# A residual pair of normalised 3x3 convolutions: another layout of the image, halos by GpSimd, another order on ScalarE, sixteen transfers per image

## The reference

```
g  = groupnorm(x), 8 groups of 2 channels, over a whole image, no affine part
k  = einsum('lj,lk,li->ijkl', u, w, v)        # 3 x 3 x 16 x 16 from three factors
x  = x + relu(conv3x3(g, k, padding SAME) + b)
```

## Time and profile before

| | before |
|---|---|
| median of 3 runs | 6190.59 us |
| the profiled execution | 6208.09 us |
| its span, first to last instruction | 6206.2 us |
| mean granted TensorE clock | 0.917 |
| HBM read, written | 268.72 MB, 268.44 MB |

### The profile page before, as it was taken

One profiled execution on the slowest core, in us unless ns is written; L12 is line 12 of the kernel. 1 busy time (PEld: TensorE's weight loads), 2 busy tenths in 40 slices (PEclk: granted clock), 3 DMA queues, 4 the chain that ended last, 5 costly groups with the idle time before them and its releaser, 6 DMA issues.

```text
span 6206.2 us, 285409 instructions
## 1 busy us (share of the span) xinstructions
PE 5071.9 (82%) x137088; PEld 2751.6 (44%) x137088; DVE 2693.6 (43%) x3084; ACT 2328.8 (38%) x3202; POOL 972.6 (16%) x453
## 2 busy tenths in 40 slices
PE   5888888888888888888888888888888878888887
PEld 3444444444444444444444444444444444444444
DVE  3444444444444444444444444444444444444443
ACT  3343343433333334334334343343433434334342
POOL 2111110111111111111111011110111101111110
PEclk9999998999999998999999899999999999999998
DMA  4454445444444445445444454454444544445424
GB/s 93 97 109 95 89 100 110 91 92 93 105 102 89 92 100 108 92 90 111 99 89 95 97 108 92 89 107 98 95 92 90 110 96 93 92 93 111 96 62 87
DMA packets 186931, 597.41 MB, mean 96 GB/s; under 512 B 13360, under 2 KB 54704, under 8 KB 185776
## 3 DMA queue, kind: packets, MB, share of 16 engines
q1 hardware_dynamic: 116144, 310.70, 23.2%
q10 hardware_dynamic: 69632, 268.45, 20.8%
HBM read 268.72 MB, written 268.44 MB: 87 GB/s over the span
## 4 chain that ended last, share of the span: by engine, by line
PE 68%; issue 19%; ACT 6%; DVE 3%; ACTq 2%; DMA 1%; POOL 0%; SPq 0%; DVEq 0%; POOLq 0%
PE ps_y L300 30%; PE ps_y L253 21%; PE ps_x L326 10%; ACT junk L356 5%; PE ps_x L281 5%; DVE odds L491 2%; ACTq L404 2%; PE ps_y L258 1%; PE ps_x L223 1%; ACT relu L374 1%; PE ps_y L261 0%; ACT relu L377 0%; PE ps_x L233 0%; DMA raw<-in_x 0%; DMA out<-pixels 0%
## 5 line engine op out<-in xcount | busy, mean ns | idle before, releaser
L300 PE MATMUL ps_y<-odds,scaled 32*32 32x512 f32 x49152 | 2021.2, 655 | 269.9 <-issue 230.3
L253 PE MATMUL ps_y<-evens,scaled 32*32 32x512 f32 x48384 | 1936.1, 638 | 350.8 <-issue 331.9
L300 PEld LDWEIGHTS ps_y<-odds,scaled 32*32 32x32 f32 x49152 | 892.4, 107 | 1163.0 <-issue 755.4
L491 DVE TENSOR_TENSOR odds<-ps_x,relu 128x2048 f32<-128x2048 f32 x256 | 586.9, 2293 | 1886.2 <-PE ps_x L281 1100.7
L253 PEld LDWEIGHTS ps_y<-evens,scaled 32*32 32x32 f32 x48384 | 927.0, 106 | 1054.4 <-issue 654.4
L491 DVE TENSOR_TENSOR result<-ps_x,relu 128x2048 f32<-128x2048 f32 x256 | 586.6, 2292 | 1314.1 <-PE ps_x L326 477.9
L211 POOL TENSOR_TENSOR fold<-fold,evens 128x1024 f32<-128x1024 f32 x384 | 843.8, 2197 | 837.4 <-DVE evens L481 800.4
L281 PE MATMUL ps_x<-evens,constants 32*32 32x512 f32 x16384 | 877.3, 652 | 117.0 <-issue 117.0
L326 PE MATMUL ps_x<-odds,constants 32*32 32x512 f32 x16384 | 838.3, 638 | 102.4 <-issue 102.2
L377 ACT ACTIVATE relu<-ps_y,bias 128x2048 f32<-128x2048 f32 x256 | 503.6, 1967 | 1070.1 <-PE ps_y L300 1070.1
L356 ACT ACTIVATE junk<-odds 128x1024 f32<-128x1024 f32 x512 | 544.4, 1063 | 928.2 <-DVE odds L491 639.4
(11 more groups left out here) (42 smaller groups left out, 1146.3 us busy)
## 6 DMA issues: line engine op xcount, KB each, us to landing
raw<-in_x SPq DMA_DIRECT2D x256, 1024.0 KB, 15.0
out<-pixels ACTq DMA_DIRECT2D x256, 1024.0 KB, 14.2
odds<-odds SPq DMA_DIRECT2D x64, 384.0 KB, 17.7
evens<-evens SPq DMA_DIRECT2D x64, 96.0 KB, 2.1
odds<-odds SPq DMA_DIRECT2D x64, 96.0 KB, 18.1
evens<-evens SPq DMA_DIRECT2D x64, 32.0 KB, 2.1
odds<-odds SPq DMA_DIRECT2D x64, 32.0 KB, 16.3
parameters<-in_params SPq DMA_DIRECT2D x2, 96.5 KB, 2.0
```

The source lines that it names most:

```text
L253: done = nc.tensor.matmul(ps_y[part, r, :], w0[rows, t * Q:(t + 1) * Q], N0[rows, k:k + EACH, i:i + H], start=(t == 0), stop=(t == NTAP - 1))
L300: done = nc.tensor.matmul(ps_y[Q * r:Q * (r + 1), q, :], w1[p % 2][Q * q:Q * (q + 1), t * Q:(t + 1) * Q], t1[Q * q:Q * (q + 1), r, k:k + E ...
L491: nc.vector.tensor_tensor(to, ps_x[:].rearrange("p q (k h) -> p q k h", h=H), R[n % R_SLOTS][:], ALU.add).then_inc(added, 1)
```

## The change

A quadrant now holds a quarter of the height: 64 rows of all 128 pairs, so `raw` has one pair of rows per partition (32 KB, contiguous in memory), `evens` is 129 slots by 66 rows and `odds` 33 slots by 258 rows. A round covers 8 slots of 64 rows in place of 2 of 256; four rounds stay. `turn_in` and `turn_out` make two transposes per round, one for each row of the pair, and write or read every second element; a ninth transpose per image brings the wrap-around slot. The halos of the evens are then rows above and below (six copies by GpSimd), those of the odds the last slot (four copies); no DMA is left in them. Padding of the evens is two instructions on 32 partitions. In the first round of conv0 four of 16 places have a slot split off. Squares are four instructions of some 2048 elements per image and kind in place of eight of 1024; on ScalarE each relu now stands ahead of the squares of its round, `pad_evens` and the roots behind a relu. There is one relu buffer, and relu waits for the add before. On VectorE `scale_weights` stands behind the add and `turn_out` of its round. Loads and stores are both issued by SP: sixteen transfers per image and direction, each over every sixteenth partition (8 partitions of 32 KB), in pieces of at most 256 elements (`max_dma_last_dim=RUN`).

```diff
+PAIRS = W // 2
+SLOTS = PAIRS // QUADS
+EACH = 8
+ROUNDS = SLOTS // EACH
+HQ = H // QUADS
+HALVES = 2
 HP = H + 2
-EACH = 2
-ROUNDS = SLOTS // EACH
-HB = H // Q
-RUN = W // QUADS * C
+HQP = HQ + 2
+WIDE = EACH * HQ
+ROW = W * C
+RUN = 256
 BANK = 512
-R_SLOTS = 2
 COUNT = H * W * 2
 NTAP = SIDES * TAPS
-FOLDS = SLOTS - 1
+FOLDS = 2 * ROUNDS - 1
+FOLD = EACH // 2
 
 PRM = Q * (1 + SIDES + TAPS) + 1
 CST = Q * (SIDES + SIDES + 1) + 2
 
-IN_DMAS, OUT_DMAS, HALO0_DMAS, HALO1_DMAS = QUADS, QUADS, 2, 3
+STRIDE = 16
+IN_DMAS, OUT_DMAS = STRIDE, STRIDE
+TURNS = HALVES * ROUNDS + 1
+HALO0, HALO1 = 2 * (QUADS - 1), QUADS
 ODDS_SUM, ODDS_PAD = 1, 2
-EVENS_SUM = 2
-EVENS_IN_A = {2: (1,), 3: (2, 3)}
-EVENS_IN_B = {0: (4,), 1: (5, 6, 7), 2: (8,)}
+EVENS_SUM, EVENS_PAD = 2, 3
 HOOK_AFTER = 2
 
 
...
 
-        raw = sb("raw", [P, HB, RUN])
-        N0 = sb("evens", [P, QUADS * SLOTS + 1, HP])
-        T1 = [sb(f"odds{i}", [P, QUADS, SLOTS + 1, HP]) for i in range(2)]
-        T2 = sb("result", [P, QUADS, EACH, H])
-        pixels = sb("pixels", [P, HB, RUN])
...
+        T1 = [sb(f"odds{i}", [P, SLOTS + 1, HP]) for i in range(2)]
+        T2 = sb("result", [P, QUADS, EACH, HQ])
+        pixels = sb("pixels", [P, HALVES, ROW])
+        R = sb("relu", [P, QUADS, WIDE])
+        fold = sb("fold", [P, QUADS, FOLD * HQ])
+        junk = sb("junk", [P, QUADS, WIDE + HQ])
         par = [sb(f"parameters{y}", [P, PRM]) for y in range(2)]
         cst = sb("constants", [P, CST])
         w_plain = [sb("weights0", [P, (2 * NTAP + 2) * Q]), sb("weights1", [P, (NTAP + 1) * Q])]
         w0 = sb("scaled0", [P, (2 * NTAP + 2) * Q])
         w1 = [sb(f"scaled1{i}", [P, (NTAP + 1) * Q]) for i in range(2)]
         mixed = sb("mixed", [P, SIDES, Q])
-        zeros = sb("zeros", [P, 2 * QUADS * (SLOTS + 1)])
-        acc = [sb(f"partial{y}", [P, SLOTS]) for y in range(2)]
+        zeros = sb("zeros", [P, PAIRS + 1])
+        acc = [sb(f"partial{y}", [P, ROUNDS]) for y in range(2)]
...
+                    pool.wait_ge(halo0, HALO0 * p + 2 * r + 1)
+                    nc.gpsimd.tensor_copy(N0[below, :, 0], N0[above, :, HQ]).then_inc(halo0, 1)
 
             def halo_of_odds(p):
-                sp.wait_ge(added, round_of(0, p, 0) + 1)
+                pool.wait_ge(added, round_of(0, p, 0) + 1)
+                pool.wait_ge(halo0, HALO0 * (p + 1))
                 t = T1[p % 2]
-                inner = slice(1, 1 + H)
-                sp.dma_start(t[0:P - Q, :, SLOTS, inner], t[Q:P, :, 0, inner]).then_inc(halo1, 16)
-                sp.dma_start(t[P - Q:P, 0:QUADS - 1, SLOTS, inner], t[0:Q, 1:QUADS, 0, inner]).then_inc(halo1, 16)
-                sp.dma_start(t[P - Q:P, QUADS - 1, SLOTS, inner], t[0:Q, 0, 0, inner]).then_inc(halo1, 16)
-
-            load(0)
+                for q in range(QUADS):
+                    of = (q + 1) % QUADS
+                    if q:
+                        pool.wait_ge(halo1, HALO1 * p + q)
+                    nc.gpsimd.tensor_copy(t[Q * q:Q * (q + 1), SLOTS, 1:1 + H],
...
+            folds(0)
             halo_of_evens(0)
-            load(1)
             for p in range(IMAGES):
                 halo_of_odds(p)
                 if p + 1 < IMAGES:
+                    folds(p + 1)
                     halo_of_evens(p + 1)
-                if p + 2 < IMAGES:
-                    load(p + 2)
-
-        @block.gpsimd
-        def _(pool):
-            nc.gpsimd.memset(zeros[:], 0.0).then_inc(zeros_set, 1)
-
-            def chunk(d):
-                return N0[:, d::SLOTS, 1:1 + H]
-
-            for p in range(IMAGES):
-                for d in range(2, SLOTS + 1):
-                    pool.wait_ge(turned_in, SLOTS * p + d)
-                    if d == 2:
-                        if p:
-                            pool.wait_ge(reduced0, p)
-                    else:
-                        pool.wait_ge(folded, FOLDS * p + d - 2)
-                    nc.gpsimd.tensor_tensor(fold[:], chunk(1) if d == 2 else fold[:], chunk(d),
-                                            ALU.add).then_inc(folded, 1)
 
         @block.tensor
...
+                            if f or q:
                                 done = nc.tensor.matmul(ps_y[part, r, :], w0[rows, t * Q:(t + 1) * Q],
-                                                        N0[rows, k:k + EACH, i:i + H],
+                                                        N0[rows, k:k + EACH, i:i + HQ],
                                                         start=(t == 0), stop=(t == NTAP - 1))
                             else:
                                 at = NTAP + 2 + t
-                                nc.tensor.matmul(ps_y[part, r, 0:H], w0[rows, at * Q:(at + 1) * Q],
-                                                 N0[rows, k, i:i + H],
+                                nc.tensor.matmul(ps_y[part, r, 0:HQ], w0[rows, at * Q:(at + 1) * Q],
+                                                 N0[rows, k, i:i + HQ],
                                                  start=(t == 0), stop=False, skip_group_check=True)
-                                nc.tensor.matmul(ps_y[part, r, H:EACH * H], w0[rows, t * Q:(t + 1) * Q],
-                                                 N0[rows, k + 1, i:i + H],
+                                nc.tensor.matmul(ps_y[part, r, HQ:WIDE], w0[rows, t * Q:(t + 1) * Q],
+                                                 N0[rows, k + 1:k + EACH, i:i + HQ],
                                                  start=False, stop=False, skip_group_check=True)
                                 if t == 0:
-                                    nc.tensor.matmul(ps_y[part, r, 0:H], w0[rows, (NTAP + 1) * Q:(NTAP + 2) * Q],
-                                                     center[0][rows, :].to_broadcast([Q, H]),
+                                    nc.tensor.matmul(ps_y[part, r, 0:HQ], w0[rows, (NTAP + 1) * Q:(NTAP + 2) * Q],
...
                             k = EACH * f + side
                             done = nc.tensor.matmul(ps_y[Q * r:Q * (r + 1), q, :],
                                                     w1[p % 2][Q * q:Q * (q + 1), t * Q:(t + 1) * Q],
-                                                    t1[Q * q:Q * (q + 1), r, k:k + EACH, i:i + H],
...
+            def stats_of_evens(p, f):
+                act.wait_ge(turned_in, TURNS * p + HALVES * (f + 1))
+                pairs = freed(f)
+                chunk = N0[:, 1:1 + PAIRS, 1:1 + HQ].rearrange("p (q k) h -> p q k h", q=QUADS)[:, :, pairs, :]
+                into = junk[:].rearrange("p q (k h) -> p q k h", h=HQ)[:, :, 0:pairs.stop - pairs.start, :]
+                square(chunk, into, acc[0][:, f:f + 1])
+
+            def stats_of_odds(p, f):
+                act.wait_ge(added, round_of(0, p, f) + 1)
+                square(T1[p % 2][:, EACH * f:EACH * (f + 1), 1:1 + H],
+                       junk[:].rearrange("p q x -> p (q x)")[:, 0:EACH * H].rearrange("p (k h) -> p k h", h=H),
...
                 if f == 0:
                     act.wait_ge(mini_read, MINI["bias", y, p] + 1)
                 act.wait_ge(y_filled, n + 1)
-                to, got = R[n % R_SLOTS][:].rearrange("p q k h -> p q (k h)"), ps_y[:]
+                if n:
+                    act.wait_ge(added, n)
                 if y == 0:
-                    ins = nc.scalar.activation(to, got, ACT.Relu, bias=bias[:, 0:1],
+                    ins = nc.scalar.activation(R[:], ps_y[:], ACT.Relu, bias=bias[:, 0:1],
                                                accum_out=acc_relu[:, f:f + 1])
                 else:
...
             def pad_evens(p):
                 act.wait_ge(scaled0, p + 1)
                 if p:
                     act.wait_ge(x_filled, round_of(0, p - 1, ROUNDS - 1) + 1)
-                slots = QUADS * SLOTS + 1
-                nc.scalar.activation(N0[:, :, 0:HP:H + 1],
-                                     zeros[:, 0:2 * slots].rearrange("p (k a) -> p k a", a=2),
-                                     ACT.Identity, bias=center[0]).then_inc(padded0, 1)
+                for part, row in ((slice(0, Q), 0), (slice(P - Q, P), HQP - 1)):
+                    ins = nc.scalar.activation(N0[part, :, row], zeros[part, :], ACT.Identity,
+                                               bias=center[0][part, :])
+                ins.then_inc(padded0, 1)
...
             for p in range(IMAGES + 1):
-                if p < IMAGES:
-                    for f in range(ROUNDS):
-                        if f:
-                            for e in range(EACH * (f - 1), EACH * f):
-                                stats_of_odds(p, e)
-                        if p + 1 < IMAGES:
-                            for d in EVENS_IN_A.get(f, ()):
-                                stats_of_evens(p + 1, d)
-                        relu(0, p, f)
-                        if f == 0 and p >= 2:
-                            store(p - 2)
-                    for e in range(SLOTS - EACH, SLOTS):
-                        stats_of_odds(p, e)
```

(63 more changed lines are left out.)

141 lines of the change are left out of this document (82 added, 59 removed).

## The result

The changed kernel takes 6802.77 us (median of 4 runs, 6797.52 to 6829.8), the kernel before 6191.68 us beside it: ratio 1.0995, 95% interval 1.0963 to 1.1026. It is 10% slower; 15% faster was forecast. The profiled execution has a span of 6795.7 us.

A forecast was written before the change was run, and what follows sets the result against it. PE was taken as bound by instructions starved in DMA bursts; afterwards DMA binds: 128 x 40.4 = 5171 us plus 2, 10, 62 and 50 idle, 5295 us of span, so 5280 us; DMA-bound range 5150 to 5500, overall 4830 to 5900.

The forecast's parts named there:

- What bounds the kernel before: PE, starved of instructions while image loads and stores burst; loss put at 19 of an image's 96 us.
- Rival D: PE is slowed by bytes moved, not turns for instructions: 19 us still lost, 5950 to 6190 us; chance 0.07.
- rival C: Instruction wait goes with time of traffic, not transfer share: 110 us an image, some 7150 us; chance 0.10.
- The transfers: Image loads and stores over 8 partitions: eight engines at 13 GB/s, 40.4 us an image each way.
- the sum: All terms together: 128 x 40.4 us of transfers plus DMA's idle time, 5295 us of span.
- The bound of DMA: Loads and stores sharing one queue need 80.8 us an image against PE's 73.2, so DMA binds.
- The turn of an instruction packet: PE's instruction packet waits behind one transfer's share; halving the share cuts 7.9 us to 3.9, under the 4.3 needed.
- rival B: Part of PE's starving stays: at 5.9 us a packet 95 us an image; placed at 5800 us; chance 0.15.
- PE's own work: PE's matmul records, 2142 + 42 an image at 30 per us, 72.8 us; 73.2 with the wait for pads.
- The split places: First round of each image's first convolution, four places split instead of one: 21 more matmuls, 1.4 us an image.
- the pads: Padding of the evens on ACT after the last relu: 0.45 us each, PE waits 0.2 to 0.5 us an image.
- The weights' scaling behind turn_out: scale_weights moved later on DVE: a whole round before its reader, so no cost.

The follow-up runs named there:

- e1: Changed kernel with transfer pieces of 1024 bytes in place of 256, still sixteen transfers of 8 partitions: 6269 us, ratio 1.0108 to the kernel before.
- e12: Kernel before with nearly all traffic left out (one transfer of 8 partitions loaded and one stored from the second image on): 5103 us.
- e5: Kernel before with each image loaded in 32 transfers of 32 partitions by 4096 bytes in place of 4, stores unchanged: 5862 us, ratio 0.9474.
- e13: Changed kernel with 1024-byte pieces and each of its sixteen transfers cut into four (8 KB per DMA engine): 5588 us, ratio 0.9028.
- e9: Changed kernel with two orders put back (reduce, pads) and eight transfers of 128 partitions by 4096 bytes per image and direction: 5323 us, ratio 0.8585.
- e10: As e9, but 32 transfers of 128 partitions by 1024 bytes (8 KB per DMA engine): 5238 us, ratio 0.8446.
- e4: Changed kernel with nearly all traffic left out (one of sixteen transfers loaded and stored from the second image on): 5382 us, ratio 0.8673.
- e11: Kernel before with loads and stores in 32 transfers of 32 partitions by 4096 bytes, stores issued by SP: 5171 us, ratio 0.8342.

## Why the prediction was wrong

**What bounds the kernel before: right.** PE starves in bursts, and the loss was well sized: 19 us an image taken, 1087/64 = 17 measured. That it is instructions that PE lacks can be read from the trace, which has the time of every DMA packet, those of the instruction queue (q8) among them. In the kernel before PE stands still for over 1 us ahead of a 512-column matmul 242 times, 771 us in all. Of these stalls 99% end between 1.2 and 1.8 us after the end of an instruction packet; of all matmuls 14% start at that distance. In e1 it is 186 stalls, 594 us, and 98%. The packets themselves take 1.10 us each in the kernel before and 1.08 in e12, so what comes late is their start. That this hangs on how the data transfers are cut, not on their bytes, is shown by e5 and e13. Rival D (by bytes) and rival C's mechanism (by the time of traffic) are out: in the changed kernel data moves nearly all the time, and its mid-round idle is 207 us against 840. C was the only rival with a slower kernel (7150 us), but for a reason that didn't come.

**The transfers: the step that failed.** "If each partition is served by one engine at today's rate per engine (208/16 = 13 GB/s), eight work, and it takes 40.4 us." Eight engines work: e1's 16,432 packets under 512 B, less 48 for parameters and constants, are 8 for each of 2048 transfers, where the kernel before has 16 (4096 for 256 stores). The Trainium skill, in "DMA: Bandwidth & Descriptors", section on the semaphore increment of 16, has a DMA use the largest number of engines up to 16 that divides the slowest dimension of both sides. The trace agrees, with 8 for 8 partitions. With 1024-byte pieces an engine also has the 13 GB/s (e1, 106 to 109 GB/s over eight). That is partly luck: 13 isn't what an engine can do, as 16 engines move 303 GB/s, 19 each, over 128 partitions (e9). But the pieces are of 256 bytes, at 10.2 GB/s an engine: 51.2 us. I read the number as elements and never weighed the piece as a price. Loads and stores take 51.74 us on average where the sum has 40.4, and 128 x 11.34 us are 1452 us of the 1501 between the span forecast, 5295 us, and the span measured, 6796. The bound of DMA that the prediction named was the right one; at 80.8 it would leave PE the lead, with the 82 us measured for it, at 103.7 it costs 10%.

**The turn of an instruction packet: mis-sized.** "Halving the 7.9 us per instruction packet gives 3.9, under the 4.3 that PE needs." No row gave that half. With a share of 32 KB in 1024-byte pieces e1's bursts run at 21.1 and 23.4 matmuls per us, so the 128 of a packet take 6.1 and 5.5 us. That is rival B's case, which put 95 us to an image at 5.9 us a packet (e1's trace has 94.7). e1 still loses 622 us in mid-round, so the forecast would have failed even with the piece that it assumed: 6269 us, not 5280. With 8 KB the stalls go (e13, e10), and over 128 partitions nearly so with 32 KB (e9). In the changed kernel itself this term is small, and hidden by the wait for DMA.

**PE's own work: 73.2 us forecast, 81.9 measured** (from image to image in e4's trace). Three parts. The rate of 30 per us gives 71.4 us for today's 2142 records, but the kernel before without traffic has 78.0: the rate was taken from rounds without the sums, in windows that also count matmuls under way. The split places take some 2 us, not 1.4; the orders take some 2, not the 0.2 to 0.5 for the pads alone. "The weights' scaling behind turn_out has a whole round before its reader" looked at the reader of the moved step and not at what is queued behind it on VectorE. With DMA at 103.7 us this can hardly show in the result.

**Small steps.** The rows by line and form after have the pads at 525 ns (0.45 taken), the evens' halo copies at 419 (0.3 to 0.5), and the strided transposes at 1278 and 1234 for 1024 elements, against 1219 and 1224 plain, so a step of two elements costs up to 5%.

```profile
L425 ACT ACTIVATE evens<-zeros,moments 32x129 f32<-32x129 f32 x128 | 67.2, 525 | 2.1 <-DVE scaled L579 1.2
L212 POOL COPY evens<-evens 32x129 f32<-32x129 f32 x192 | 80.4, 419 | 16.3
L506 DVE STREAM_TRANSPOSE evens<-raw 128x1024 f32<-128x1024 f32 x256 | 316.9, 1278 | 0.0
```

By subtraction the 611 us split so: the traffic costs the kernel before 1087 us (e12) and the changed one 6803 - 5382 = 1421 (e4), 334 more; the rest of the change costs 279. But the costs don't simply add: in the changed kernel the 279 us lie within the time that DMA takes anyway.

## What to carry to other kernels

Where PE streams long code beside bulk transfers, count what one transfer gives each DMA engine, and try transfers cut until that is about 8 KB, at the same bytes. Here that took mid-round idle from 840 to 112 us in the layout before (e11, where the stores also changed queue) and from 622 to 56 us in the new one (e1 to e13). Let a transfer cover all 128 partitions where the layout allows: it is over sooner, and starves PE less even with 32 KB (e9). Check the unit and the price of a piece before a transfer is cut into pieces: 256-byte ones cost nearly a quarter of the rate. And when a step is moved back in an engine's queue, look at who waits for the next step in that queue.
